# Nine instead of eight source tiles with a complement mask in the second attention of a two-layer graph network

## The chip, the cores and the metric

The kernel runs on one core of a Trainium2 chip. TensorE (PE in the profile) multiplies matrices, VectorE (DVE) and ScalarE (ACT) work elementwise, GpSimd (POOL) and SyncE (SP) mostly start transfers. The metric is the device time of one execution in microseconds. Lower is better.

## What is computed

Two attention layers run over a graph of 2048 nodes with 512 features. The change lies in the second one, which in the reference reads, cut to what matters:

```
seq = (x @ W_seq).reshape(N, H, DH)            # N 2048, H 16 heads, DH 32
score1 = einsum('nhd,d->hn', seq, a1); score2 = einsum('nhd,d->hn', seq, a2)
scores = leaky_relu(score1[:, :, None] + score2[:, None, :], 0.2)
scores = scores + (1.0 - adj)[None] * MASK_VAL  # only neighbours count
attn = softmax(scores, axis=-1)
hidden = einsum('hij,jhd->ihd', attn, seq).reshape(N, 512)
return elu(hidden @ W_out + b_out)
```

## The kernel before

The program is a series of blocks, each a hand-written order for every engine with semaphores between them: projections of the first layer, its attention (L1172 is near its end), a short block that prepares scores (L1181 to L1284), the second attention (stage 4), and the output projection (L1555 to L1644). The change touches stage 4 and the two preparations that serve it (L1168, L1220).

**How stage 4 works.** The leaky ReLU has two slopes, and which of them counts for target i and source j depends on the sign of score1[i] + score2[j]. So the exponential factors into per-target and per-source terms in each of the two cases, and a head needs no exponential per pair: it needs, for each source, a sum over neighbours on one side of the sign and a sum over neighbours on the other side. The 2048 sources are 16 tiles j of 128. Per head n and tile j:

- ScalarE (L1350) writes a sign mask of 128 sources by 2048 targets in fp8. For tiles 3, 8 and 13 VectorE does it (L1390).
- VectorE (`mask`, L1399) ands it in place with the adjacency tile: neighbours on the first side.
- If j is in `FAR`, VectorE also (`far`, L1404) xors the adjacency tile with this mask: neighbours on the other side, the complement mask.
- TensorE (`step`) multiplies. The values V are bf16 in three parts of 66 columns, 33 for each side. A tile in `FAR` takes for 128 targets one matmul of 99 columns with the mask as weights (L1500) and one of 99 columns with the complement mask (L1501). A tile not in `FAR`, a near tile, takes one of 198 columns with the mask (L1503) and one of 99 columns with a negated adjacency tile (L1504), and the signs that the first layer's block and the score block put there make the sum the same.

A step does eight such pairs for one half of the targets, a half-step below. PE does half 1 of tile j four tiles (`LAG`) behind half 0, so its order in a head is (0,0), (0,1), (0,2), (0,3), (0,4), (1,0), (0,5), (1,1), (0,6), (1,2), ..., (0,15), (1,11), and then (1,12) to (1,15), with the half first and the tile second.

**What ties the engines together.** PE may begin half 0 of a head when VectorE has taken half 0 of the head before out of PSUM (`bank_free[0]`, given by `sum_parts`, L1415, which VectorE does behind mask 3), and half 1 after the second L1415, behind mask 5. `sum_parts` itself waits until PE has ended that half (`psum_done`). ScalarE may overwrite mask j of the head before when PE has used it (`mask_used`). ScalarE's packing of the next head's values (L1339, ahead of its sign 10 and of its sign 15) waits for PE to end the head before. `values(n + 1)` (L1370, L1373) and `take_off` (L1385) prepare the next head's V on VectorE, and are left out in head 15. There is one buffer of 16 masks, and one complement mask for each tile in `FAR`.

The negated adjacency tiles are made once by L1168 at the end of the first attention, and the sign of a far tile's values is set by GpSimd memsets at L1220.

Of the kernel before, what the change touches and what calls it, by code (L numbers as in the profile page):

```python
# [18 lines left out]
U32 = mybir.dt.uint32  # L19
U8 = mybir.dt.uint8  # L20
F8 = mybir.dt.float8e4
# [5 lines left out]
N = 2048  # L27
D = 512
NT = N // P
# [20 lines left out]
DZ = DH + 1  # L50
# [1128 lines left out]
def stage3(nc, c, io, t, s, ps):  # L1179
# [25 lines left out]
    with nc.Block() as block:  # L1205
# [9 lines left out]
        def _(pool):  # L1215
            pool.memset(shift[:, :], SHIFT).then_inc(consts, 1)
            pool.memset(sign[:, :, :], 1.0).then_inc(consts, 1)
            pool.wait_ge(consts, 2)
            for j in FAR:
                pool.memset(sign[:, 1, j:j + 1], -1.0).then_inc(consts, 1)  # L1220
# [3 lines left out]
        def _(dve):  # L1224
# [26 lines left out]
            dve.tensor_scalar(t["s2"][:, :, 1, :], s2, -1.0, None, ALU.mult).then_inc(t["lasting"], 1)  # L1251
            dve.wait_ge(consts, 3 + len(FAR))
            dve.tensor_tensor(scale[:, :, :], sign[:, :, :], rstd[:, None, :].to_broadcast([P, 2, NT]), ALU.mult).then_inc(scaled, 1)
# [21 lines left out]
        def _(pe):  # L1275
# [6 lines left out]
            pe.wait_ge(peaked, 2)  # L1282
            pe.wait_ge(consts, 3 + len(FAR))
            pe.matmul(ps[:, 3, 0:HB], ones[0:HB, :], peaks[0:HB, :], start=True, stop=True).then_inc(top_all, 1)  # L1284
# [2 lines left out]
HALF = N // 2  # L1287
HT = HALF // P
VECTOR_SIGN = (3, 8, 13)
FAR = (0, 3, 5, 7, 9, 11, 13, 14)  # L1290
NEAR_TILES = tuple(j for j in range(NT) if j not in FAR)
NS = NT - len(VECTOR_SIGN)
LAG = 4
CZ = 2 * DZ


def stage4(nc, c, io, t, s, ps):
# [5 lines left out]
    V = sb("V", [P, 2, NT, 3, CZ], BF16)  # L1303
    tmp = sb("tmp", [P, 2, NT, CZ])
    upper = tmp[:, :, :, :].bitcast(BF16).rearrange("p s j (c w) -> p s j c w", w=2)[:, :, :, :, 1]
    masks, fars, s1b = t["masks"], t["fars"], t["s1b"]
# [11 lines left out]
    with nc.Block() as block:  # L1318
# [41 lines left out]
        def _(dve):  # L1360
# [40 lines left out]
            def far(n, j):  # L1401

                dve.wait_ge(mask_ready, NT * n + j + 1)
                dve.tensor_tensor(fars[:, FAR.index(j), :].bitcast(U32).rearrange("p (t i) -> p t i", t=NT),  # L1404
                                  adjT[:, :, j, :].bitcast(U32),
                                  masks[:, j, :].bitcast(U32).rearrange("p (t i) -> p t i", t=NT), ALU.bitwise_xor
                                  ).then_inc(far_ready, 1)
# [34 lines left out]
            def head(n, b):  # L1442
                for j in range(NT):
                    if j + 1 in VECTOR_SIGN:
                        vector_sign(n, b, j + 1)
                    mask(n, j)
                    if j - 1 in FAR:
                        far(n, j - 1)
# [33 lines left out]
        @block.tensor  # L1482
        def _(pe):
            pe.sem_inc(mask_used, NT - 1)

            def step(n, b, half, j):

                base = 4 * half
                if j == 0:
                    pe.wait_ge(bank_free[half], n + 1)  # L1490
                pe.wait_ge(mask_ready, NT * n + j + 1)
                if j in FAR:
                    pe.wait_ge(far_ready, len(FAR) * n + FAR.index(j) + 1)
                for i in range(HT):
                    cols = slice(half * HALF + i * P, half * HALF + (i + 1) * P)
                    out = ps[:, base + i // 2, 256 * (i % 2):256 * (i % 2) + 3 * CZ].rearrange("p (s c) -> p s c", s=3)
                    first = dict(start=(j == 0 and i % 2 == 0), stop=False, skip_group_check=True)
                    then = dict(start=False, stop=(j == NT - 1), skip_group_check=True)
                    if j in FAR:
                        pe.matmul(out[:, :, 0:DZ], masks[:, j, cols], V[:, b, j, :, 0:DZ], **first)  # L1500
                        last = pe.matmul(out[:, :, DZ:CZ], fars[:, FAR.index(j), cols], V[:, b, j, :, DZ:CZ], **then)  # L1501
                    else:
                        pe.matmul(out, masks[:, j, cols], V[:, b, j, :, :], **first)  # L1503
                        last = pe.matmul(out[:, :, DZ:CZ], nadjT[:, NEAR_TILES.index(j), cols], V[:, b, j, :, DZ:CZ], **then)  # L1504
                if j == NT - 1:
                    last.then_inc(psum_done[half], 1)
                if half and j < NT - 1:
                    last.then_inc(mask_used, 1)

            def head(n, b):  # L1510
                pe.wait_ge(split, n + 1)
                pe.wait_ge(packed, 2 * (n + 1))
                for j in range(NT):
                    step(n, b, 0, j)
                    if j >= LAG:
                        step(n, b, 1, j - LAG)
                for j in range(NT - LAG, NT):
                    step(n, b, 1, j)
            for n in range(HB):
                head(n, n % 2)  # L1520
# [127 lines left out]
def build(nc, io, out, kind="Internal"):  # L1648
    dram = lambda name, shape, dt=F32: nc.dram_tensor(name, shape, dt, kind=kind).ap()
    t = {  # L1650
        "rel_planes": [dram(f"rel_planes{i}", [NE, NE], U8) for i in range(PLANES)], "x1": dram("x1", [N, D]),
        "s1_rows": dram("s1_rows", [HB, N]), "seq_rows": dram("seq_rows", [N, D]),
        "adj_chunks": dram("adj_chunks", [NT, P, N], F8),
    }
    with ExitStack() as c:
        t["ident"] = c.enter_context(nc.sbuf_tensor("ident", [P, P], F32))
        t["identb"] = c.enter_context(nc.sbuf_tensor("identb", [P, P], BF16))
        t["offdiag"] = c.enter_context(nc.sbuf_tensor("offdiag", [P, P], BF16))
        t["offdiag8"] = c.enter_context(nc.sbuf_tensor("offdiag8", [P, P], F8))
        ps = c.enter_context(nc.psum_tensor("psum", [P, 8, 512], F32))  # L1660
        s = {n: c.enter_context(nc.semaphore(n)) for n in ("zeroed", "const", "const8", "lasting")}
        t["lasting"] = s["lasting"]
        t["adjT_in"], t["seq_in"] = (c.enter_context(nc.semaphore(n)) for n in ("adjT_in", "seq_in"))
        t["rstd"] = c.enter_context(nc.sbuf_tensor("rstd", [P, 2, NT], F32))
        t["mv"] = c.enter_context(nc.sbuf_tensor("mv", [P, NT, 2], F32))
        t["sc"] = c.enter_context(nc.sbuf_tensor("scores", [P, 2, HB, NT], F32))

        area_a, area_b = (c.enter_context(nc.sbuf_tensor(f"area_{n}", [P, 2 * KT * NE], F32)) for n in "ab")
        late = c.enter_context(nc.sbuf_tensor("late", [P, max((2 * PLANES + 5) * NE // 4, 2 * KT * D)], F32))
        t["nadjT"] = late[:, 0:len(NEAR_TILES) * N // 4].bitcast(F8).rearrange("p (j i) -> p j i", i=N)  # L1670
        area_h = c.enter_context(nc.sbuf_tensor("area_h", [P, NT * D], F32))
        t["h"] = area_h[:, :].rearrange("p (t d) -> p t d", t=NT)
        t["adjT"] = area_a[:, 0:NT * N // 4].bitcast(F8).rearrange("p (t j i) -> p t j i", t=NT, j=NT)
        t["s1b"] = area_a[:, NT * N // 4:].rearrange("p (b i) -> p b i", b=2)
        t["seq"] = area_b[:, 0:NT * D].rearrange("p (t d) -> p t d", t=NT)
        t["fars"] = area_b[:, NT * D:].bitcast(F8).rearrange("p (j i) -> p j i", i=N)
        t["masks"] = area_h[:, :].bitcast(F8).rearrange("p (j i) -> p j i", i=N)
        with ExitStack() as first:
            f = FirstLayer(nc, first, area_a, area_b, late)
            with ExitStack() as part:  # L1680
                stage1(nc, part, io, t, s, ps, f)
            with ExitStack() as part:
                stage2(nc, part, io, t, s, ps, f)
        with ExitStack() as second:
            sb = lambda name, shape, dt=F32: second.enter_context(nc.sbuf_tensor(name, shape, dt))
            t["wout"], t["bout"] = sb("wout", [P, KT, D]), sb("bout", [P, D])
            t["wout_in"] = second.enter_context(nc.semaphore("wout_in"))
            with ExitStack() as attention:
                sb = lambda name, shape, dt=F32: attention.enter_context(nc.sbuf_tensor(name, shape, dt))
                t["s2"] = sb("s2", [P, HB, 2, NT])  # L1690
                t["e"], t["er"], t["sign"] = sb("e", [P, 2, NT, HB]), sb("er", [P, 2, NT, HB]), sb("sign", [P, 2, NT])
                t["w"] = sb("w", [P, HB, NT, 2])
                with ExitStack() as part:
                    stage3(nc, part, io, t, s, ps)
                with ExitStack() as part:
                    stage4(nc, part, io, t, s, ps)
            with ExitStack() as part:
                stage5(nc, part, io, out, t, s, ps)
# [20 lines left out]
```

## Time and profile before

| what | value |
|---|---|
| time, median of 3 runs (lowest, highest) | 1215.81 us (1212.07, 1216.4) |
| time of the profiled execution | 1213.02 us |
| span of the profiled execution | 1211.4 us |
| granted TensorE clock, mean | 0.974 |
| busy: PE, DVE, ACT | 1103.5, 950.3, 808.1 us |

The span runs from the first to the last instruction. Busy time is a sum over the whole program, whose stages have different limits. A row of a timeline has its start, its duration, the engine, the line and its output and inputs. Successive VectorE instructions overlap: each is shown longer than the distance from its start to the next start, so the pace of an engine is read from starts.

### The profile page before, as it was taken

The numbers are of one execution on the slowest core, as the hardware profiler recorded it, in microseconds if no ns is written. First come the engines' busy times: TensorE is split into PE (matmuls) and PEld (weight loads), VectorE is DVE, ScalarE is ACT, GpSimd is POOL, SyncE is SP. The second block draws the span as 40 slices with busy tenths as digits, with TensorE's granted clock in tenths as the row PEclk, the third lists the DMA queues.
The fourth block names the chain that finished last, engine by engine and source line by source line (L and its number), as shares of the span: only waits on it lengthen the run. The fifth ranks groups of instructions, "written<-read, shape, count | busy, mean of one in ns | idle before, by whom it ended". The sixth has DMA issues, their size and how long they took to land. (4 is left out here: it accounts for less than half of the span.)

```text
span 1211.4 us, 24794 instructions
## 1 busy us (share of the span) xinstructions
PE 1103.5 (91%) x10565; PEld 765.7 (63%) x10565; DVE 950.3 (78%) x1320; ACT 808.1 (67%) x844; POOL 124.7 (10%) x143
## 2 busy tenths in 40 slices
PE   4799796999999999999895799999999999999897
PEld 3344343444444444444442799999999999999643
DVE  2381145999999999998833799999999999999365
ACT  1334236666667776666522999998999999997022
POOL 3677550000000000000000000000000000000011
PEclk9899897999999999999997899999999999999899
DMA  9530443222222121000431111010111111100311
GB/s 352 113 25 1 106 103 81 55 46 64 63 64 62 41 43 39 33 35 27 165 122 68 64 50 55 37 37 37 37 37 37 38 37 37 38 37 2 136 73 70
DMA packets 35213, 77.69 MB, mean 64 GB/s; under 512 B 5669, under 2 KB 10658, under 8 KB 33058
## 3 DMA queue, kind: packets, MB, share of 16 engines
q1 hardware_dynamic: 27314, 60.55, 14.2%
q0 software_dynamic: 7792, 15.58, 7.3%
q8 instruction: 84, 1.38, 0.5%
q14 instruction: 23, 0.19, 0.1%
HBM read 65.39 MB, written 23.21 MB: 73 GB/s over the span
## 5 line engine op out<-in xcount | busy, mean ns | idle before, releaser
L1350 ACT ACTIVATE area_h<-area_a,s 128x2048 fp8e4<-128x2048 f32 x208 | 396.9, 1987 | 5.0 <-DMA area_a<-s_rows 5.0
L1503 PE MATMUL psum<-s_V,area_h 128*128 128x198 bf16 x2048 | 285.5, 248 | 0.0
L1504 PE MATMUL psum<-s_V,late 128*128 128x99 bf16 x2048 | 279.5, 208 | 0.0
L1500 PE MATMUL psum<-s_V,area_h 128*128 128x99 bf16 x2048 | 206.1, 210 | 18.3 <-DVE area_b L1404 17.7
L1501 PE MATMUL psum<-s_V,area_b 128*128 128x99 bf16 x2048 | 206.0, 209 | 0.0
L1500 PEld LDWEIGHTS psum<-s_V,area_h 128*128 128x128 fp8e4 x2048 | 189.5, 98 | 19.0 <-issue 17.1
L1503 PEld LDWEIGHTS psum<-s_V,area_h 128*128 128x128 fp8e4 x2048 | 199.3, 97 | 0.1
L1504 PEld LDWEIGHTS psum<-s_V,late 128*128 128x128 fp8e4 x2048 | 199.4, 97 | 0.0
L1501 PEld LDWEIGHTS psum<-s_V,area_b 128*128 128x128 fp8e4 x2048 | 189.7, 98 | 0.0
L1399 DVE TENSOR_TENSOR area_h<-area_h,area_a 128x512 uint32<-128x512 uint32 x256 | 171.6, 686 | 14.4 <-ACT area_h L1350 10.0
L1119 DVE CUSTOM_DVE_ANT_0 area_b<-psum,late 128x1500 f32<-128x1500 f32 x96 | 161.2, 1717 | 26.8 <-PE psum L629 17.1
L714 PE MATMUL psum<-area_h,s_WT 128*128 128x512 f32 x384 | 181.6, 598 | 0.0
L1108 DVE SCALAR_TENSOR_TENSOR s_W<-area_b,s_r,s_W 128x1500 f32<-128x1500 f32 x96 | 170.8, 1779 | 2.2
L916 ACT ACTIVATE area_b<-area_b,s_negm 128x1500 f32<-128x1500 f32 x96 | 147.7, 1539 | 19.7 <-DVE s_negm L1119 19.6
L629 PE MATMUL psum<-area_a 64*128 64x512 f32 (+1 forms) x576 | 141.0, 605 | 6.5 <-DVE s_negm L1119 6.4
L146 POOL DMA_INDIRECT rel_planes<-f_ones,f_flat x80 | 99.4, 1242 | 61.2 <-DMA rel_planes<-s_zero 24.1
L714 PEld LDWEIGHTS psum<-area_h,s_WT 128*128 128x128 f32 x384 | 66.9, 190 | 55.9 <-issue 55.4
L629 PEld LDWEIGHTS psum<-area_a 64*128 64x128 f32 x576 | 55.4, 189 | 67.0 <-issue 55.1
L425 PE MATMUL psum<-s_hT,s_wT 128*128 128x512 f32 x192 | 85.4, 604 | 6.6 <-ACT area_a L375 2.9
L1404 DVE TENSOR_TENSOR area_b<-area_a,area_h 128x512 uint32<-128x512 uint32 x128 | 87.7, 685 | 0.0
L862 ACT ACTIVATE s_WT<-psum 128x256 f32<-128x256 f32 x96 | 36.2, 377 | 53.4 <-PE psum L684 29.7
L425 PEld LDWEIGHTS psum<-s_hT,s_wT 128*128 128x128 f32 x192 | 36.7, 193 | 52.1 <-issue 47.8
(169 smaller groups left out, 1172.0 us busy)
## 6 DMA issues: line engine op xcount, KB each, us to landing
area_a<-s_rows SPq DMA_DIRECT2D x16, 1024.0 KB, 4.8
rel_planes<-s_zero POOLq DMA_DIRECT2D x3, 2304.0 KB, 23.0
late<-rel_planes SPq DMA_DIRECT2D x36, 192.0 KB, 2.6
area_h<-in_x SPq DMA_DIRECT2D x4, 1024.0 KB, 20.3
f_adj<-in_adj POOLq DMA_DIRECT2D x16, 256.0 KB, 6.1
s_x<-in_x SPq DMA_DIRECT2D x16, 256.0 KB, 2.7
x<-s_x SPq DMA_DIRECT2D x16, 256.0 KB, 2.0
area_a<-adj_chunks SPq DMA_DIRECT2D x4, 1024.0 KB, 9.2
```

The costliest lines, as they stand in the source:

```text
L425: last = pe.matmul(ps[:, 4 + g % 4, :], wT[w][:, k, dt * P:(dt + 1) * P], hT[:, k, ch * 512:(ch + 1) * 512], start=(k == 0), stop=(k == KT ...
L629: return pe.matmul(ps[:, 3 * half + ch, 0:cols.stop - cols.start], qk[rows, Q, p, r * P:(r + 1) * P], qk[rows, K, p, cols], start=True, st ...
L714: last = pe.matmul(ps[:, 7 if r < ET - 1 else 0, :], WT[m % 2][:, b, :], h[:, 2 * m + b, :], start=(m == order[0] and b == 0), stop=(m == ...
L916: act.activation(ex[:, hd, 0:NREL], ex[:, hd, 0:NREL], ACT.Exp, bias=negm[:, b, hd:hd + 1], scale=-1.0, accum_out=zs[:, b, hd:hd + 1]).the ...
L1108: dve.scalar_tensor_tensor(w, ex[:, hd, 0:NREL], r8[:, hd:hd + 1], w, ALU.mult, ALU.add).then_inc(added if hd < HA - 1 else w_ready, 1)
L1119: dve.tensor_tensor_reduce(ex[:, hd, 0:NREL], ps[:, 3 * (hd % 2):3 * (hd % 2) + 3, :].rearrange("p c j -> p (c j)")[:, 0:NREL], low[r % 2] ...
L1350: act.activation(masks[:, j, :], s1b[:, b, :], ACT.Relu, bias=t["s2"][:, n, 0, j:j + 1], scale=BIG, saturate=False).then_inc(signs, 1)
L1399: dve.tensor_tensor(own, own, adjT[:, :, j, :].bitcast(U32), ALU.bitwise_and).then_inc(mask_ready, 1)
L1500: pe.matmul(out[:, :, 0:DZ], masks[:, j, cols], V[:, b, j, :, 0:DZ], **first)
L1501: last = pe.matmul(out[:, :, DZ:CZ], fars[:, FAR.index(j), cols], V[:, b, j, :, DZ:CZ], **then)
L1503: pe.matmul(out, masks[:, j, cols], V[:, b, j, :, :], **first)
L1504: last = pe.matmul(out[:, :, DZ:CZ], nadjT[:, NEAR_TILES.index(j), cols], V[:, b, j, :, DZ:CZ], **then)
```

## The change

`FAR` goes from eight tiles to nine: tile 6 joins. The list of near tiles loses it and has seven, so that one negated adjacency tile fewer is made and its memory, in `late`, is free. That memory takes the ninth complement mask. As the masks are numbered by their place in `FAR`, it is tile 14 whose complement mask now lies there, and tile 6 uses the fourth place in `area_b`.

```diff
-FAR = (0, 3, 5, 7, 9, 11, 13, 14)
+FAR = (0, 3, 5, 6, 7, 9, 11, 13, 14)
 NEAR_TILES = tuple(j for j in range(NT) if j not in FAR)
...
-                dve.tensor_tensor(fars[:, FAR.index(j), :].bitcast(U32).rearrange("p (t i) -> p t i", t=NT),
+                dve.tensor_tensor(fars[FAR.index(j)].bitcast(U32).rearrange("p (t i) -> p t i", t=NT),
...
-                        last = pe.matmul(out[:, :, DZ:CZ], fars[:, FAR.index(j), cols], V[:, b, j, :, DZ:CZ], **then)
+                        last = pe.matmul(out[:, :, DZ:CZ], fars[FAR.index(j)][:, cols], V[:, b, j, :, DZ:CZ], **then)
...
-        t["fars"] = area_b[:, NT * D:].bitcast(F8).rearrange("p (j i) -> p j i", i=N)
+        fars = area_b[:, NT * D:].bitcast(F8).rearrange("p (j i) -> p j i", i=N)
+        t["fars"] = [fars[:, i, :] for i in range(8)] + [late[:, len(NEAR_TILES) * N // 4:(len(NEAR_TILES) + 1) * N // 4].bitcast(F8)]
```

VectorE's order in a head of stage 4, from the mask of tile 5 to the mask of tile 9, before (L1399 is a mask, L1404 a complement mask, L1390 the sign of tile 8, L1415 the second sum):

```order
L1399 TENSOR_TENSOR area_h<-area_h,area_a 128x512
L1415 TENSOR_REDUCE s_sums<-psum 128x528
L1399 TENSOR_TENSOR area_h<-area_h,area_a 128x512
L1404 TENSOR_TENSOR area_b<-area_a,area_h 128x512
L1390 TENSOR_SCALAR area_h<-area_a,s 128x2048
L1399 TENSOR_TENSOR area_h<-area_h,area_a 128x512 x2
L1404 TENSOR_TENSOR area_b<-area_a,area_h 128x512
L1399 TENSOR_TENSOR area_h<-area_h,area_a 128x512
```

and the same place of the changed kernel:

```order
L1399 TENSOR_TENSOR area_h<-area_h,area_a 128x512
L1415 TENSOR_REDUCE s_sums<-psum 128x528
L1399 TENSOR_TENSOR area_h<-area_h,area_a 128x512
L1404 TENSOR_TENSOR area_b<-area_a,area_h 128x512
L1390 TENSOR_SCALAR area_h<-area_a,s 128x2048
L1399 TENSOR_TENSOR area_h<-area_h,area_a 128x512
L1404 TENSOR_TENSOR area_b<-area_a,area_h 128x512
L1399 TENSOR_TENSOR area_h<-area_h,area_a 128x512
L1404 TENSOR_TENSOR area_b<-area_a,area_h 128x512
L1399 TENSOR_TENSOR area_h<-area_h,area_a 128x512
```

One complement mask, that of tile 6, stands between the masks of tiles 7 and 8. Nothing else of VectorE's order in the head moved. On PE, the end of half-step (1,1) and the start of (0,6) before:

```order
L1503 MATMUL psum<-s_V,area_h 128x198
L1504 MATMUL psum<-s_V,late 128x3x33
L1503 MATMUL psum<-s_V,area_h 128x198
L1504 MATMUL psum<-s_V,late 128x3x33
L1503 MATMUL psum<-s_V,area_h 128x198
L1504 MATMUL psum<-s_V,late 128x3x33
```

and of the changed kernel:

```order
L1503 MATMUL psum<-s_V,area_h 128x198
L1504 MATMUL psum<-s_V,late 128x3x33
L1503 MATMUL psum<-s_V,area_h 128x198
L1504 MATMUL psum<-s_V,late 128x3x33
L1500 MATMUL psum<-s_V,area_h 128x3x33
L1501 MATMUL psum<-s_V,area_b 128x3x33
```

The two half-steps of tile 6 turn from the near form into the far form, with as many matmuls in the same order.

## Rows read from the trace of the kernel before

**Rows 1.** The page's busy shares, in all and in 40 slices.

```profile
PE 1103.5 (91%) x10565; PEld 765.7 (63%) x10565; DVE 950.3 (78%) x1320; ACT 808.1 (67%) x844; POOL 124.7 (10%) x143
...
PE   4799796999999999999895799999999999999897
...
DVE  2381145999999999998833799999999999999365
```

**Rows 2.** The waits of all engines from 706 to 1120 us: total, times, longest.

```profile
ACT s_V L1339 <- PE psum L1504: 20.0, 11, 1.9
DVE s_sums L1415 <- PE psum L1504: 3.1, 10, 0.9
```

**Rows 3.** Windows over head 9 and over head 3.

```profile
core 0: us, PE busy (x) PEld busy (x) DVE busy (x) ACT busy (x) POOL busy (x), PEclk, DMA share, GB/s
923.88:952.40 28.52, 28.52 (x515) 28.52 (x513) 27.98 (x39) 26.68 (x16) 0.00 (x0) 1.00 0.10 39
753.93:782.15 28.22, 28.22 (x510) 28.22 (x508) 27.89 (x39) 28.12 (x17) 0.00 (x0) 1.00 0.10 38
```

**Rows 4.** VectorE's timeline in head 9, around the two sums.

```profile
923.88 1.29 DVE L1399 TENSOR_TENSOR area_h<-area_h,area_a 128x512 uint32<-128x512 uint32 x2
...
925.69 1.22 DVE L1370 TENSOR_TENSOR s_tmp<-area_b,er 128x1024 f32<-128x1024 f32 x1
...
926.95 1.28 DVE L1390 TENSOR_SCALAR area_h<-area_a,s 128x2048 fp8e4<-128x2048 f32 x1
...
931.29 0.69 DVE L1399 TENSOR_TENSOR area_h<-area_h,area_a 128x512 uint32<-128x512 uint32 x1
931.90 0.68 DVE L1404 TENSOR_TENSOR area_b<-area_a,area_h 128x512 uint32<-128x512 uint32 x1
932.50 0.68 DVE L1399 TENSOR_TENSOR area_h<-area_h,area_a 128x512 uint32<-128x512 uint32 x1
933.39 1.81 DVE L1415 TENSOR_REDUCE s_sums<-psum 128x528 f32<-128x1584 f32 x1 [0.21 <-PE psum L1504]
935.35 0.69 DVE L1399 TENSOR_TENSOR area_h<-area_h,area_a 128x512 uint32<-128x512 uint32 x1
...
937.76 1.29 DVE L1399 TENSOR_TENSOR area_h<-area_h,area_a 128x512 uint32<-128x512 uint32 x2
938.96 0.69 DVE L1404 TENSOR_TENSOR area_b<-area_a,area_h 128x512 uint32<-128x512 uint32 x1
```

**Rows 5.** PE's timeline: two far half-steps from 860.42, two near ones from 861.91.

```profile
860.42 0.21 PE L1500 MATMUL psum<-s_V,area_h 128*128 128x99 bf16 x1
...
861.91 0.25 PE L1503 MATMUL psum<-s_V,area_h 128*128 128x198 bf16 x1
...
864.00 0.21 PE L1500 MATMUL psum<-s_V,area_h 128*128 128x99 bf16 x1
```

**Rows 6.** VectorE's timeline in heads 0 and 1, where it waits for ScalarE.

```profile
683.94 1.25 DVE L1385 TENSOR_TENSOR s_tmp<-s_tmp 128x1056 f32<-128x1056 f32 x1
685.77 0.69 DVE L1399 TENSOR_TENSOR area_h<-area_h,area_a 128x512 uint32<-128x512 uint32 x1 [0.58 <-ACT area_h L1350]
...
698.11 0.69 DVE L1399 TENSOR_TENSOR area_h<-area_h,area_a 128x512 uint32<-128x512 uint32 x1 [1.20 <-ACT area_h L1350]
...
702.97 1.80 DVE L1415 TENSOR_REDUCE s_sums<-psum 128x528 f32<-128x1584 f32 x1
704.91 0.69 DVE L1399 TENSOR_TENSOR area_h<-area_h,area_a 128x512 uint32<-128x512 uint32 x1
```

**Rows 7.** PE's timeline: the end of head 0, the start of head 1, and its last matmul of stage 4.

```profile
704.18 0.21 PE L1504 MATMUL psum<-s_V,late 128*128 128x99 bf16 x1
705.04 0.21 PE L1500 MATMUL psum<-s_V,area_h 128*128 128x99 bf16 x1 [0.65 <-issue]
...
1132.80 0.21 PE L1504 MATMUL psum<-s_V,late 128*128 128x99 bf16 x1
```

**Rows 8.** VectorE's timeline: negated tiles and what follows; later, what waits behind GpSimd's memsets.

```profile
612.71 2.77 DVE L1168 TENSOR_SCALAR late<-area_a 128x512 uint32<-128x512 uint32 x8
620.16 0.69 DVE L1063 TENSOR_TENSOR s_x<-s_x,psum 128x512 f32<-128x512 f32 x1 [4.68 <-PE psum L714]
...
655.39 0.22 DVE L1242 TENSOR_SCALAR s_peaks<-ident,s_peak 16x16 f32<-16x16 f32 x1
...
656.31 0.42 DVE L1247 TENSOR_TENSOR s_d<-s_sc,psum 128x256 f32<-128x256 f32 x1 [0.50 <-PE psum L1284]
```

**Rows 9.** GpSimd's timeline in the score block.

```profile
653.30 0.33 POOL L1220 MEMSET sign<- 128x1 f32 x8
653.56 0.20 POOL L1221 MEMSET s_ones<- 128x128 f32 x1
```

## The prediction, made before the changed kernel ran

> **What bounds the kernel now.** The page's slices came first [rows 1]. Both PE and DVE stand at nine tenths through the slices of stage 4, from about 670 to 1133 us, so this stage has two candidates for its limit. A share cannot say which, so I went to the waits of the stage [rows 2]. The reader is to see that DVE waits for PE ten times and only 3.1 us in all, that ScalarE waits for PE but nobody waits for ScalarE, and that PE does not appear. Last, the starts of single instructions, which give a pace that durations hide.
>
> A late head takes 28.52 us and an early one 28.22 us [rows 3]. Both are heads with the same instructions. In the early head DVE runs without a wait, so 28.22 us is what DVE needs. In the late one it starts the mask behind which the second sum stands at 932.50, could start the sum 0.60 later, at 933.10, and starts it at 933.39 because PE has not ended the head before [rows 4]. That is 0.29 us of waiting, and 28.52 - 0.29 = 28.23 agrees. PE's pace follows from its first matmul of head 1 at 705.04 and its last at 1132.80: with 0.05 for the last pair's rest, 427.81 us for 15 heads, or 28.52 us a head with nothing between [rows 7]. **So PE limits the stage at 28.52 us a head, and DVE has 0.30 us a head to spare.** DVE could run ahead for the first heads and then was held back. This margin decides the case.
>
> **What PE gains.** Two far half-steps take 861.91 - 860.42 = 1.49 us, two near ones 864.00 - 861.91 = 2.09 us [rows 5]. Tile 6 has two half-steps in a head, which turn from near to far: 0.60 us less. PE then needs 28.52 - 0.60 = 27.92 us a head.
>
> **What DVE pays.** One more L1404 in each head. It is shown as 0.68 to 0.69 us, but from its start at 931.90 the next instruction follows at 932.50: it occupies 0.60 us of the order [rows 4]. DVE then needs 28.22 + 0.60 = 28.82 us a head. That is above PE's old 28.52 and well above PE's new 27.92, so DVE becomes the limit, and a head costs 0.30 us more than before. If its shown duration of 0.69 us were its price instead, a head would need another 0.09 us, and the sum below 13 x 0.09 = 1.2 us more. The Trainium skill, "VectorE: DVE Perf Modes", section on the TRN2 errata, prices a tensor_tensor of 512 fp32 elements at (512 + 151)/0.96 = 691 ns; the row's duration agrees with it, the distance between starts does not. I keep the starts, since they repeat at 931.29, 931.90 and 932.50.
>
> **Is DVE then really never held?** Take T as the start of the mask behind the first sum (931.29 in head 9). PE starts half 0 at T + 0.13, as 705.04 stands to 704.91 in head 1 [rows 6, 7].
> - Up to (0,6) PE has eight half-steps, four far and four near: 4 x 0.745 + 4 x 1.045 = 7.16, so it wants the new complement mask at T + 7.29. DVE without its wait starts the mask of tile 7 at T + 6.18 (937.76 - 0.29 - 931.29) and the new L1404 at T + 6.78, and ends it at T + 7.47. PE waits some 0.2 us there, a new wait.
> - PE ends the head at T + 0.13 + 27.92 + 0.2 = T + 28.25. The next T comes at T + 28.82. PE waits 0.57 + 0.13 = 0.7 us at each head's start, for the first sum.
> - The second sum is due 1.8 us behind the new T, when PE has been done for 2.4 us: the old wait of 0.29 us goes. The first sum needs PE's end of half 0, which is T + 28.25 less the last five half-steps (11 to 15: three far, two near, 4.3 us), T + 23.9. DVE comes to it at about T + 26.9 (28.82 less the sum's 1.94). Not held.
> - ScalarE was busy 26.68 of 28.52 us and nobody waited for it [rows 2, 3]. Its wait for PE comes 0.6 us earlier against DVE's order than T does. Not held either.
>
> **The sum.** Heads 0 and 1 up to 698.11 are paced by ScalarE: DVE waits for its signs. In head 0 the new L1404 comes ahead of the L1385 at 683.94, which would start at 684.54 and be done with 1.17 later at 685.71, while the next mask waits for ScalarE until 685.77 [rows 6]. The 0.60 us is swallowed there, and 698.11 stays, and with it T of head 1 at 704.91. From there DVE paces: T of head 14 is 704.91 + 13 x 28.82 = 1079.57. PE ends head 14 at 1079.57 + 28.25 = 1107.82. In head 15 DVE has no next values to prepare, 925.69 to 926.95 = 1.26 us less ahead of T [rows 4], so its T is 1107.13, earlier than PE's end, and PE goes straight on: 1107.82 + 27.92 = 1135.74. Before it was 1132.80 + 0.05 = 1132.85. **Stage 4 ends 2.9 us later**, and what follows hangs on PE's end in both kernels.
>
> The other parts cost nothing. One of eight L1168 goes (0.33 us), but DVE then sits idle 4.68 us until PE, so nothing comes of it; were that cover gone it would be 0.3 us gained. One more memset at L1220 is 0.03 us on GpSimd (653.30 to 653.56 for eight), whose last memset starts at 653.56, while the matmul it holds back, L1284, also needs DVE's L1242 of 655.39 and ends only near 656.3 [rows 8, 9]. Writing tile 14's mask into `late` rather than `area_b` has no row. The same sizes in another place could cost nothing, or at the most what a sum from PSUM shows beyond its duration, 1.94 - 1.80 = 0.14 us a head, 2 us in all. I take nothing, as L1168 writes `late` at the plain pace of its kind.
>
> The profiled execution would go from 1213.02 to 1215.9 us. The median of the runs shown is 2.8 us above that execution, so against the median I predict 1215.81 + 2.9 = 1218.7 us.
>
> **The rivals.**
> 1. *PE's relief counts, the kernel gets faster.* PE busy stands at the full 28.52 us of a head, weight loads too, and DVE at 27.98 [rows 3]. The Trainium skill, "Perfetto Trace Analysis", section Identifying the Most-Contended Engine, says to optimise the engine with the highest occupancy first. By rows that would mean 15 heads less 0.60 us each: 9.0 us less, 1206.8 us. It needs DVE to have more than 0.60 us a head to spare, and it has 0.30. And the new L1404 would have to be felt by less than that margin. Chance 4 in 100.
> 2. *The whole xor is paid.* If DVE keeps some wait of about 0.3 us while it is the limit, because a hand-over to PE or ScalarE shifts with it, a head costs 0.60 us more: 15 x 0.60 = 9.0, 1224.8 us. Against it are the 2.4 and 3 us of room above. Chance 6 in 100.
> 3. *PE's new pauses lower its clock.* The clock reads 1.00 in stage 4 and PE never rests there. It paused 0.86 us at 704.18 without losing the clock in the heads that follow (1.00 in head 3) [rows 3, 7]. As DVE limits, PE would have to lose over 0.7 of 27.9 us, more than 2.5%, before it cost anything; at 5% it would cost another 0.7 us a head, some 10 us, 1229 us. Chance 3 in 100.
> 4. *Nothing comes of it.* DVE's margin is used up exactly: if the new L1404 overlapped its neighbours more, at 0.30 us, the time stays 1215.8 us. Nothing in the rows has such a pace for this form. Chance 5 in 100.
>
> **How the numbers follow.** My forecast has 82 in 100. Within 0.5% (6.1 us) is about what a measurement of this kernel can tell from no change; its three runs lie 4.3 us apart. +2.9 us is inside, and with such a scatter some 8 of the 82 land beyond +6.1. Slower by over 0.5%: 8 + 6 + 3 = 17. Faster: 4. Same: 74 + 5 = 79. The range reaches down over rival 4 with the scatter and up over the dearer price (1.2 us) and `late` (2 us): 1213.5 to 1223.5. The two ends at 9 us stay outside.
>
> **What would show it.** Right: starts of the same DVE instruction 28.82 us apart from head to head; no wait of L1415 for PE between heads 2 and 14; a PE gap of 0.7 us at L1500 at each head's start and one of 0.2 us ahead of tile 6; 144 L1404; the last matmul of the stage at 1135.7. The relief side is right if PE's busy stretch per head is 27.9. Wrong: heads of 28.5 us or less, a DVE wait for signs or for PE that stays, an L1404 that writes `late` at another pace, a clock below 1.00 in the stage.

## The result

The changed kernel took 1217.64 us (median of 22 runs, 1215.36 to 1221.19) against 1215.43 us for the kernel before in as many runs (1212.07 to 1218.91). The medians lie 2.2 us apart. The ratio is 1.0025, with a 95% interval of 1.0014 to 1.0035: slower by 3.0 us (1.7 to 4.3 us), and less than 0.5%. The forecast was 1218.7 us, 2.9 us more than before. The profiled execution took 1215.61 us with a span of 1214.0.

The page of the changed kernel, busy shares and the same slices as in [rows 1]:

```profile
PE 1096.9 (90%) x10565; PEld 754.7 (62%) x10565; DVE 958.4 (79%) x1335; ACT 809.7 (67%) x844; POOL 123.7 (10%) x144
...
PE   4799787999999999999894899999999999999897
...
DVE  2381246999999999998833799999999999999465
```

The page hardly shows what happened: PE lost 6.6 us of busy time, DVE gained 8.1, and the slices read nearly alike. The windows over heads 3 and 10 show it:

```profile
core 0: us, PE busy (x) PEld busy (x) DVE busy (x) ACT busy (x) POOL busy (x), PEclk, DMA share, GB/s
754.56:783.38 28.82, 28.22 (x517) 27.89 (x514) 28.49 (x39) 26.79 (x16) 0.00 (x0) 1.00 0.11 39
956.26:985.08 28.82, 28.21 (x516) 27.88 (x514) 28.49 (x39) 26.78 (x16) 0.00 (x0) 1.00 0.11 41
```

An early and a late head now last the same 28.82 us, where there were 28.22 and 28.52 [rows 3]. PE, which had filled its heads, has a hole in each. Its weight loads fill 27.88 us. The waits of the stage from 762 to 1100 us, total, times, longest:

```profile
ACT s_V L1339 <- DVE s_tmp L1385: 24.1, 12, 2.0
PEld psum L1500 <- issue: 11.2, 24, 0.6
PE psum L1500 <- issue: 5.1, 12, 0.5
PE psum L1500 <- DVE area_b L1404: 2.0, 11, 0.2
```

The reader is to see that they have changed sides. The row of DVE's L1415 waiting for PE [rows 2] is gone, PE and its weight loads (PEld) have rows where they had none, and ScalarE waits for DVE's L1385 where it had waited for PE. DVE in head 9, around the sums and tile 6, against [rows 4]:

```profile
932.90 1.80 DVE L1415 TENSOR_REDUCE s_sums<-psum 128x528 f32<-128x1584 f32 x1
934.85 0.69 DVE L1399 TENSOR_TENSOR area_h<-area_h,area_a 128x512 uint32<-128x512 uint32 x1
935.46 0.69 DVE L1404 TENSOR_TENSOR area_b<-area_a,area_h 128x512 uint32<-128x512 uint32 x1
936.06 0.69 DVE L1399 TENSOR_TENSOR area_h<-area_h,area_a 128x512 uint32<-128x512 uint32 x1
936.66 1.80 DVE L1415 TENSOR_REDUCE s_sums<-psum 128x528 f32<-128x1584 f32 x1
...
941.01 0.69 DVE L1399 TENSOR_TENSOR area_h<-area_h,area_a 128x512 uint32<-128x512 uint32 x1
941.62 0.69 DVE L1404 TENSOR_TENSOR area_b<-area_a,area_h 128x512 uint32<-128x512 uint32 x1
942.22 0.69 DVE L1399 TENSOR_TENSOR area_h<-area_h,area_a 128x512 uint32<-128x512 uint32 x1
```

The second sum follows its mask by 0.60 us, with no wait. The new L1404 at 941.62 occupies 0.60 us. PE in the same head, at its start and ahead of tile 6, and its last matmul of the stage:

```profile
934.34 0.21 PE L1504 MATMUL psum<-s_V,late 128*128 128x99 bf16 x1
934.97 0.21 PE L1500 MATMUL psum<-s_V,area_h 128*128 128x99 bf16 x1 [0.42 <-issue]
...
942.06 0.21 PE L1504 MATMUL psum<-s_V,late 128*128 128x99 bf16 x1
942.46 0.21 PE L1500 MATMUL psum<-s_V,area_h 128*128 128x99 bf16 x1 [0.19 <-DVE area_b L1404]
...
1135.15 0.21 PE L1504 MATMUL psum<-s_V,late 128*128 128x99 bf16 x1
```

PE starts 0.12 us behind the mask at 934.85, which follows the first sum. From start to start its holes are 0.63 and 0.40 us, less the usual 0.05: 0.58 us at the head's start and 0.35 at tile 6.

Stage 4, from its first mask (667.71 before, 666.77 now) to its last matmul (1132.80, 1135.15), took 465.1 us before and 468.4 now, 3.3 more. The place where the stage begins moves by some microseconds from one profile to the next (666.5 to 674.2 us in the fourteen profiles of this study), with work ahead of it that is the same but for the negated tiles. So below I read the distance between heads and the length of the stage beside the ratio of the times. Both are in the table.

| kernel | FAR | heads apart, us | stage 4, us, against before | ratio to before, 95% interval |
|---|---|---|---|---|
| before | 8 | 28.22, then 28.52 | 465.1 | 1 |
| changed | 9 | 28.82 | +3.3 | 1.0025 [1.0014, 1.0035] |
| e1_cost | 8, one xor more | 28.82 | +3.8 | 1.0029 [1.0012, 1.0046] |
| e2_gain | 9, one xor less | 28.21 | -5.3 | 0.995 [0.9932, 0.9968] |
| e4_ten | 10 | 29.42 | +10.4 | 1.0081 [1.0049, 1.0113] |
| e3_tile12 | 9, tile 12 in place of 6 | 28.82 | +3.0 | none, a single run of 1218.24 us |
| e5_before_pool | 8, values on GpSimd | 28.78 | +2.5 | 1.0028 [1.0008, 1.0049] |
| e6_after_pool | 9, values on GpSimd | 29.38 | +9.2 | 1.0074 [1.0042, 1.0106] |
| e8_pool_ten | 10, values and scaling | 30.57 | +26.4 | 1.0217 [1.0175, 1.0259] |
| e7_pool2_eleven | 11, values and scaling | 31.17 | +35.1 | 1.0295 [1.0252, 1.0338] |
| e9_after_timed | 9, values, timed | 27.63, then 27.89 | -10.3 | 0.9937 [0.9917, 0.9958] |
| e10_before_timed | 8, values, timed | 28.52 | -0.8 | 1.0002 [0.9988, 1.0016] |
| e11_ten_timed | 10, values and scaling, timed | 28.83 | +3.4 | 1.0038 [1.0023, 1.0054] |
| e12_ten_values | 10, values, timed | 28.24 | -6.1 | 0.9947 [0.9929, 0.9964] |

"Values" and "scaling" are pieces of DVE's work given to GpSimd, and "timed" means that GpSimd waits for a chosen place in DVE's order before it starts them. The medians of the kernel before lay between 1214.48 and 1216.55 us in these comparisons. One of the twelve executions of e1_cost took 6455.91 us and is left out of its ratio.

### The profile page after: what moved, and what is told of

Read it like the earlier page. It is cut to its first block and busy times, and to the rows that moved or that the text cites. A ratio compares the mean times of both kernels' runs of the same rounds, so it can differ in the third digit from the quotient of the medians.

```text
span 1214.0 us, 24842 instructions
## 1 busy us (share of the span) xinstructions
PE 1096.9 (90%) x10565; PEld 754.7 (62%) x10565; DVE 958.4 (79%) x1335; ACT 809.7 (67%) x844; POOL 123.7 (10%) x144
## 5 line engine op out<-in xcount | busy, mean ns | idle before, releaser
L1500 PE MATMUL psum<-s_V,area_h 128*128 128x99 bf16 x2304 | 231.5, 209 | 26.8 <-DVE area_b L1404 20.6
L1503 PE MATMUL psum<-s_V,area_h 128*128 128x198 bf16 x1792 | 254.0, 248 | 0.0
L1504 PE MATMUL psum<-s_V,late 128*128 128x99 bf16 x1792 | 247.4, 208 | 0.0
L1399 DVE TENSOR_TENSOR area_h<-area_h,area_a 128x512 uint32<-128x512 uint32 x256 | 172.8, 686 | 14.5 <-ACT area_h L1350 9.8
L1504 PEld LDWEIGHTS psum<-s_V,late 128*128 128x128 fp8e4 x1792 | 174.8, 98 | 0.0
L1404 DVE TENSOR_TENSOR area_b<-area_a,area_h 128x512 uint32<-128x512 uint32 x128 | 87.6, 684 | 0.0
```

Of the source, the lines that this page charges most:

```text
L1399: dve.tensor_tensor(own, own, adjT[:, :, j, :].bitcast(U32), ALU.bitwise_and).then_inc(mask_ready, 1)
```

## The experiments

**The two halves apart.** The theory: PE and DVE each have a need per head, the larger one sets the pace, and the ninth tile takes 0.60 us from one and gives 0.60 us to the other. The rivals: PE alone counts, or DVE's xor is paid whole.

e1_cost, one part alone, the xor:

```diff
+            def extra(n, j):
+                dve.wait_ge(mask_ready, NT * n + j + 1)
+                if n > 0:
+                    dve.wait_ge(spared, n)
+                dve.tensor_tensor(spare[:, :]..., adjT[:, :, j, :]..., masks[:, j, :]..., ALU.bitwise_xor).then_inc(spared, 1)
...
+                    if j == 7:
+                        extra(n, 6)
```

> The kernel before, with one more xor of tile 6 on VectorE in each head, behind the mask of tile 7, into a tile of its own that nobody reads. TensorE's work is that of before. Theory (VectorE's margin of 0.30 us a head is overrun): VectorE needs 28.82 us a head, TensorE 28.52, so heads start 28.82 us apart; the first sum of head 14 ends at 704.91 + 13 x 28.82 = 1079.57, TensorE ends head 14 at 1079.57 + 0.13 + 28.52 = 1108.22 and head 15 at 1136.7: 3.9 us slower than before, ratio 1.003, and about 1 us slower than the change. Rival (TensorE is the limit and hides the xor): 0 us, ratio 1.000. Rival (the whole xor is paid): 9.0 us, ratio 1.007.

Measured: heads 28.82 us apart, stage 4 3.8 us longer, ratio 1.0029. DVE waits for nothing from head 2 on, and PE has one hole of about 0.3 us a head. That is the theory's 3.9 us, and it excludes both rivals. The stage is 0.5 us longer than the changed kernel's and not 1 us, since the changed kernel has a pause of 0.37 us that e1 has not (last section).

e2_gain, the other part alone:

```diff
-                    if j - 1 in FAR:
+                    if j - 1 in FAR and j - 1 != 6:
                         far(n, j - 1)
...
+                        other = adjT[:, half * HT + i, j, :] if j == 6 else fars[FAR.index(j)][:, cols]
+                        last = pe.matmul(out[:, :, DZ:CZ], other, V[:, b, j, :, DZ:CZ], **then)
```

> The changed kernel without the xor of tile 6: the second matmul of tile 6 takes the plain adjacency tile as weights in place of the complement mask, which leaves that part of the sum out. TensorE has the relief, VectorE does not pay. Theory (two engines, each with its own need): VectorE needs 28.22 us a head as before, TensorE 27.92, so heads start 28.22 us apart from head 1 to head 14 and stage 4 ends at 704.91 + 13 x 28.22 + 0.13 + 2 x 27.92 = 1127.7, which is 5.1 us faster than before, ratio 0.996. Rival (TensorE's relief counts in full): 15 x 0.60 = 9.0 us faster, ratio 0.9926.

Measured: heads 28.21 us apart in all of the stage, 5.3 us shorter, ratio 0.995. So of PE's 0.60 us a head only 0.31 can be had, because DVE then stands at its own 28.22. In its waits from 740 to 1100 us, PE and ScalarE wait and DVE never does:

```profile
ACT s_V L1339 <- DVE s_tmp L1385: 12.5, 11, 1.2
PEld psum L1500 <- issue: 4.0, 12, 0.5
ACT s_V L1339 <- PE psum L1505: 3.3, 11, 0.4
PE psum L1500 <- issue: 1.9, 10, 0.3
```

**A tenth tile** (`FAR = (0, 3, 5, 6, 7, 9, 11, 12, 13, 14)`).

> The changed kernel with a tenth tile, 12, in FAR, whose complement mask takes the memory of another negated adjacency tile. Theory (VectorE is the limit since the ninth): the whole 0.60 us of this xor is paid now, 29.42 us a head, and head 15 is held by VectorE too, so TensorE ends stage 4 at 704.91 + 13 x 29.42 + 29.42 - 1.26 + 0.13 + 27.6 = 1143.3: 10.4 us slower than before, ratio 1.0086, that is 7.5 us more than the ninth tile cost. Rival (each tile costs the same): some 6 us slower than before, ratio 1.005.

Measured: 29.42 us and +10.4 us in the stage, as worked out. The ninth tile cost 3.3 us and the tenth 7.1: the first was half paid out of the margin, the second was paid whole. It is the 29.42 us from head to head that tells this from the rival. The interval of the ratio, 1.0049 to 1.0113, hardly does, as the rival's 1.005 lies at its edge.

**Another ninth tile** (12 in place of 6).

> The ninth tile of FAR is 12 in place of 6. Theory: at tile 6 TensorE waits 0.2 to 0.4 us for the complement mask in each head, and at tile 12, where it is further behind VectorE, it does not; but this wait lies in TensorE's spare time, so TensorE waits that much longer at the head's start instead, heads stay 28.82 us apart and the end moves by less than 0.4 us. Rival (the wait at tile 6 is part of the cost): 0.34 us a head less, some 5 us faster than the change.

PE's hole at the head's start is now 0.9 us on the average and there is no other (waits of PE from 740 to 1100 us):

```profile
PEld psum L1500 <- issue: 11.4, 12, 1.2
PE psum L1500 <- issue: 9.4, 12, 1.0
```

Heads stay 28.82 us apart and the stage is 0.3 us shorter than the change's. The wait at tile 6 cost nothing but that. A single run stands behind this, so it rests on the trace and not on the time.

**Giving DVE room, first try.** If DVE is the limit with nine tiles, taking 1.26 us a head off DVE must be worth a lot there and nothing with eight. `values` for heads 1 to 15 went to GpSimd, and in e8 and e7 the scaling of the sums as well, which starts there once the second sum is done:

```diff
+        @block.gpsimd
+        def _(pool):
+            for n in range(HB):
+                if n < HB - 1:
+                    values(pool, n + 1)
...
-                        if j == 1:
-                            values(n + 1)
```

> The kernel before (eight tiles in FAR) with the next head's values (L1370 and L1373, 1.26 us of VectorE's order a head) on GpSimd, which is idle in stage 4. Theory: VectorE's need falls to 26.96 us a head, but TensorE keeps its 28.52 us and is the limit, so VectorE only waits longer for it at L1415 (1.5 us a head in place of 0.29) and the time stays: ratio 1.000. Rival (VectorE's time counts whenever it is busy): 15 x 1.26 = 19 us faster at most, ratio 0.984. Rival (GpSimd and VectorE hinder each other): slower, VectorE's starts further apart while GpSimd works.

> The changed kernel (nine tiles) with the next head's values on GpSimd. Theory: VectorE needs 28.82 - 1.26 = 27.56 us a head, less than TensorE's 27.92, so TensorE is the limit again and its relief comes out in full: heads 27.92 us apart, 15 x 0.60 = 9.0 us faster than before, ratio 0.9926, that is 12 us faster than the change. The same edit that is worth nothing on the kernel before is worth 12 us here. Rival (hindrance between GpSimd and VectorE, unknown size): heads over 27.9 us apart, with L1399 or L1390 over their 0.60 and 1.19 us.

> Ten tiles in FAR (6 and 12 joined), with the next head's values and the scaling of the sums (L1423, 1.17 us of VectorE's order) on GpSimd. Theory: VectorE 29.42 - 1.26 - 1.17 = 26.99 us a head, TensorE 28.52 - 1.20 = 27.32, ScalarE 26.7: TensorE limits, 15 x 1.2 = 18 us faster than before, ratio 0.985. Rival (ScalarE, now nearly full, holds the heads, or GpSimd hinders VectorE): 27.9 us a head or more, at most 9 us faster.

> As the run with ten tiles and two pieces on GpSimd, but eleven tiles in FAR (2, 6 and 12 joined). Theory: VectorE 27.59 us a head, TensorE 26.72: VectorE is the limit again, heads 27.6 us apart, 13 to 14 us faster than before, ratio 0.989, slower than with ten tiles. Rival (the eleventh tile still pays): faster than with ten tiles.

The four expectations are, in this order, those of e5, e6, e8 and e7. All four came out slower than the theory said, by 2.5 to 49 us of the stage. The rival about hindrance had it in the first three, and for e7 no rival had it. GpSimd and DVE in one head of e6_after_pool, the two rows of GpSimd ahead of five of DVE:

```profile
802.97 4.66 POOL L1324 TENSOR_TENSOR s_tmp<-area_b,er 128x1024 f32<-128x1024 f32 x1 [23.48 <-DVE s_tmp L1385]
807.58 1.28 POOL L1327 TENSOR_TENSOR s_tmp<-e,sign 128x32 f32<-128x32 f32 x1
```

```profile
803.34 0.68 DVE L1404 TENSOR_TENSOR area_b<-area_a,area_h 128x512 uint32<-128x512 uint32 x1
803.95 0.68 DVE L1399 TENSOR_TENSOR area_h<-area_h,area_a 128x512 uint32<-128x512 uint32 x1
804.55 1.25 DVE L1385 TENSOR_TENSOR s_V<-s_tmp 128x1056 bf16<-128x1056 f32 x1
805.71 2.99 DVE L1390 TENSOR_SCALAR area_h<-area_a,s 128x2048 fp8e4<-128x2048 f32 x1
808.63 0.78 DVE L1399 TENSOR_TENSOR area_h<-area_h,area_a 128x512 uint32<-128x512 uint32 x1
```

The L1390 that comes while GpSimd works takes 2.92 us to the next start, not 1.19. That is 1.72 us more, with 0.1 on the mask behind it: 27.56 + 1.82 = 29.38, the measured distance, and with eight tiles 26.96 + 1.82 = 28.78, also as measured. In e8 a second instruction a head is held, the mask that comes when GpSimd scales (its line is L1404 in that kernel, and it is shown with 2.45 us in place of 0.68): 26.99 + 1.8 + 1.8 = 30.6. With e7's eleventh tile 0.60 more gives 31.2. So the theory of two needs stands, with DVE's need mis-sized by the hold.

Not every DVE instruction under GpSimd is held. Those at 803.34, 803.95 and 804.55 ran at their usual 0.60 and 1.17 us from start to start, although GpSimd had been at work since 802.97, and it was GpSimd's own instruction that became longer: 4.66 us, where e9 below shows 2.35. The heads of e5, e6 and e8 repeat this. Which of the two gives way, and when, these runs do not settle.

The Trainium skill, "GPSIMD Engine Reference", section Specifications, lists SBUF interfaces that GpSimd shares with VectorE, in contention with VectorE instructions in a mode that uses two ports, or with two inputs in SBUF. The rows agree that the two engines hinder each other, and that a mask with its two SBUF inputs can be held (2.45 us). But the three at 803.34 to 804.55 have two SBUF inputs as well and were not. Whether L1390 runs in such a mode no row shows; it has one input and takes 1.19 us for 2048 elements, while L1385 with two takes 1.17 us for 1056.

**Second try: out of each other's way.** GpSimd starts the values behind the mask of tile 2:

```diff
+                    pool.wait_ge(mask_ready, NT * n + 3)
                     values(pool, n + 1)
```

> The changed kernel with the next head's values on GpSimd, as in the run before, but GpSimd starts them only behind VectorE's mask of tile 2. There VectorE has no L1390 for 8.4 us, longer than GpSimd's 5.9 us. Theory (what went wrong was one L1390 a head that stood until GpSimd's instruction ended, 2.91 us in place of 1.19): VectorE's need is 27.56 us a head, TensorE's 27.92 limits, heads 27.92 us apart, 15 x 0.60 = 9.0 us faster than the first kernel, ratio 0.9926. Rival (GpSimd slows VectorE's other instructions too, or the hand-over costs): heads over 28 us apart, ratio above 0.995.

> The same edit on the first kernel, with eight tiles in FAR. Theory: TensorE's 28.52 us limits with or without it, so nothing changes: ratio 1.000, VectorE waits some 1.5 us a head for TensorE at L1415. Rival (VectorE's time is worth something in the first kernel too): some 0.3 us a head faster or more, ratio 0.997 or less.

With nine tiles the ratio is 0.9937, the heads end 27.89 us apart, and DVE waits for PE again. PE's need of 27.92 us is met to 0.03 us. The first heads are 27.63 us apart, which is DVE's need of 27.56 and 0.07 more on the mask that follows the sum, until PE holds DVE back. The stage is 10.3 us shorter and not 9.0: 0.8 us of that come from head 1, which PE begins 0.8 us earlier, in e10 too, and the rest from the 0.03 us a head. With eight tiles the same edit is worth nothing: 1.0002. DVE only waits there, in the rows from 720 to 1100 us of e10, where the kernel before had waited 3.1 us in its stage [rows 2]:

```profile
DVE s_sums L1415 <- PE psum L1509: 16.9, 25, 0.9
```

GpSimd and DVE in a head of e9, under the first sum:

```profile
844.95 2.35 POOL L1324 TENSOR_TENSOR s_tmp<-area_b,er 128x1024 f32<-128x1024 f32 x1 [25.02 <-DVE area_h L1399]
```

```profile
845.39 1.80 DVE L1415 TENSOR_REDUCE s_sums<-psum 128x528 f32<-128x1584 f32 x1
847.33 0.77 DVE L1399 TENSOR_TENSOR area_h<-area_h,area_a 128x512 uint32<-128x512 uint32 x1
```

GpSimd's instruction takes 2.35 us here, not 4.66, and the sum keeps its 1.94 us to the next start. It falls under the sum, whose only input lies in PSUM. That was luck: I had chosen the place for having no L1390. What was measured is the pair of places; that the sum's PSUM input is what makes them agree is argued.

**More tiles in that form.**

> Ten tiles in FAR (6 and 12 joined), the next head's values on GpSimd behind the mask of tile 2, and the scaling of the sums on GpSimd behind the mask of tile 7, where VectorE has no L1390 for some 6 us and GpSimd needs 2. Theory: VectorE 26.99 us, TensorE 27.32 us a head, TensorE limits: 15 x 1.2 = 18 us faster than the first kernel, ratio 0.985. Rival (ScalarE, 26.7 us a head, or a hand-over becomes the limit): heads 27.6 us apart or more, ratio above 0.989.

> Ten tiles in FAR with the next head's values on GpSimd behind the mask of tile 2, and the scaling of the sums back on VectorE. Theory (in the run with both pieces on GpSimd the scaling there held one L1404 of VectorE for 1.78 us a head, more than the 1.17 us that it took off VectorE): VectorE needs 29.42 - 1.26 + 0.07 = 28.23 us a head, which is 0.6 us less than the 28.83 of that run though it has more to do, and it limits (TensorE 27.3): stage 4 some 6 us shorter than in the first kernel, ratio 0.995. Rival (the hold at L1404 comes from the ten tiles and not from GpSimd's scaling): the long L1404 stays and heads are 30 us apart, ratio over 1.01.

The two expectations are those of e11_ten_timed and e12_ten_values. e11 missed by 1.5 us a head. One L1404 (the masks' line in that kernel) stands while GpSimd scales:

```profile
854.03 2.45 DVE L1404 TENSOR_TENSOR area_h<-area_h,area_a 128x512 uint32<-128x512 uint32 x1
856.41 0.68 DVE L1409 TENSOR_TENSOR area_b<-area_a,area_h 128x512 uint32<-128x512 uint32 x1
```

```profile
853.59 2.34 POOL L1332 TENSOR_TENSOR s_sums<-s_sums,w 128x1056 f32<-128x1056 f32 x1 [6.79 <-DVE area_h L1404]
```

2.38 us from start to start is 1.78 too many, and 26.99 + 1.78 + 0.07 = 28.84 against 28.83 measured. e12, which gives the scaling back to DVE, does more on DVE and is faster: 28.24 for 28.23 expected, 0.9947. The mask at that place follows at the usual pace again, so the hold came from GpSimd's scaling and not from the ten tiles. The interval of e12 overlaps that of e9, but its heads are 0.35 us longer, so nine tiles and the values on GpSimd is the best kernel measured: 0.6% faster than the kernel before.

## Why the prediction was right, by its steps

- *PE limits at 28.52 us with 0.30 us to spare on DVE.* Shown: e10 gives DVE 1.26 us more room and the heads stay 28.52 us apart.
- *PE gains 0.60 us a head.* Shown: weight loads of 27.88 us a head in the changed kernel and 27.89 us heads in e9, against 27.92 worked out.
- *DVE pays 0.60, not 0.69, and becomes the limit at 28.82.* Shown by 28.82 from head to head, in the change and in e1, by 28.21 without the xor in e2, and by 29.42 with ten. The price by duration would have given 28.91.
- *PE waits 0.2 us at tile 6 and 0.7 at the head's start.* 0.35 and 0.58 measured, 0.93 together for the 0.9 of the forecast. The wait at tile 6 was sized too small: the forecast let PE start when the new L1404 ends, and PE starts 0.15 us behind it (941.62 + 0.69 = 942.31, and 942.46). The wait at the head's start absorbs what this one takes, as e3 shows.
- *Heads 0 and 1 swallow the new xor.* The mask that had waited for ScalarE at 685.77 comes 18.06 us behind the stage's first one in both kernels, and the mask at 698.11 comes 30.40 us behind it in both.
- *The sum, +2.9 us.* The stage grew by 3.3. Of the 0.4 us more, DVE is already 0.3 us late when it comes to T of head 14 (412.15 us behind the stage's first mask, 411.86 in the forecast), by a pause of 0.37 us in head 2 that no step foresaw (below). The other 0.1 us comes behind it, where PE waits longer at tile 6 than forecast. The interval of the ratio, 1.7 to 4.3 us, cannot tell 2.9 from 3.3; that the sum holds term by term rests on the traces. The median came out 1.1 us below the 1218.7 of the forecast, less than what the kernel's executions scatter.
- *Rivals.* PE's relief in full (0.9926), the whole xor (1.0074) and no change (1.000) all lie outside the change's own interval, and e1 and e2 exclude the first two as well. The granted clock reads 1.00 from 674.9 to 1130 us in both kernels, in spite of PE's new holes. The forecast's sentence that it reads 1.00 in stage 4 and that PE never rests there was not right for the start: from 667.0 to 674.2 us it reads 0.50 in both kernels (the level of 1.2 GHz), with PE busy for only 2.18 and 3.12 of these 7.2 us. This lies in head 0, and head 1 begins 28.50 us behind the stage's first mask in both kernels. `late` as a place cost nothing: L1404 into it is followed 0.60 us later by the next instruction, as into `area_b`.

## What to carry to other kernels

When two engines both look full, measure the need of each from the starts of its instructions in a stretch in which it waits for nothing, and count a move of work against the margin between the two needs. Here 0.30 us of the first 0.60 were covered by the margin, and of the next 0.60 nothing. No run moved a piece that fits within the margin whole. A move that does not pay can still be half of one that does. Nine tiles cost 0.25%, GpSimd's help alone gave nothing, and both together gave 0.6%.

Work given to an idle engine must be placed, too. With nine tiles, the same edit left the kernel 0.7% slower or made it 0.6% faster than the one before, by when GpSimd started its piece.

## What the runs showed that I had not expected

- A tensor_tensor on GpSimd held one DVE instruction by 1.7 to 1.8 us in each head, and the larger one of the values (128x1024 fp32) itself took 4.66 us in place of 2.35. L1390 and a mask were held, but three two-input instructions of DVE that fell under the longer GpSimd instruction were not, nor was a sum out of PSUM.
- DVE paused for 0.37 us behind the first sum of head 2 in the changed kernel and in e3, at the same instruction, and in no other kernel. The trace puts the wait to ScalarE, whose sign mask had been written over 5 us earlier. The same two kernels have a second such pause, of 0.35 us, behind the second sum of head 15, where it delays nothing. The cause stays open. The rows of both pauses in the changed kernel:

```profile
730.84 1.80 DVE L1415 TENSOR_REDUCE s_sums<-psum 128x528 f32<-128x1584 f32 x1
733.15 0.69 DVE L1399 TENSOR_TENSOR area_h<-area_h,area_a 128x512 uint32<-128x512 uint32 x1 [0.52 <-ACT area_h L1350]
...
1108.30 1.80 DVE L1415 TENSOR_REDUCE s_sums<-psum 128x528 f32<-128x1584 f32 x1
1110.60 0.69 DVE L1399 TENSOR_TENSOR area_h<-area_h,area_a 128x512 uint32<-128x512 uint32 x1 [0.50 <-DVE s_sums L1415]
```
